# The place of the key norms and the row sums between two pairs of heads, in a decoder layer on one core

## The reference

```
P = layernorm(x) @ W_in + b_in            # 16 heads of Q, K, V, G, 64 wide each
W = (1e-4 + sqrt(max(q2 + k2 - 2 Q K^T, 0))) ** -2    # q2, k2: squared norms
W = W / (1e-4 + sum(W, axis=-1))
H = G * (W @ V)
x = x + H @ W_out + b_out
```

## Time and profile before

| what | value |
|---|---|
| median of 3 runs | 1544.21 us (1541.64 to 1545.7) |
| the profiled execution | 1542.54 us, its span 1540.7 us |
| granted TensorE clock, mean over the span | 0.961 |
| busy: PE, DVE, ACT, POOL | 1389.6, 995.6, 925.9, 600.9 us |
| row sums (L592) | 128 instructions, 32.7 us |
| key norms (L511) into `ps_s` | 240 instructions, 29.6 us |

### The profile page before, as it was taken

One profiled execution on the slowest core, in us unless ns is written; L12 is line 12 of the kernel. 1 busy time (PEld: TensorE's weight loads), 2 busy tenths in 40 slices (PEclk: granted clock), 3 DMA queues, 4 the chain that ended last, 5 costly groups with the idle time before them and its releaser, 6 DMA issues.

```text
span 1540.7 us, 22759 instructions
## 1 busy us (share of the span) xinstructions
PE 1389.6 (90%) x7209; PEld 878.4 (57%) x7210; DVE 995.6 (65%) x1447; ACT 925.9 (60%) x678; POOL 600.9 (39%) x484
## 2 busy tenths in 40 slices
PE   6899999999999999999989558888872999999995
PEld 4555555555555555555546146676661666666664
DVE  7978888888888988898885826666666221212121
ACT  1789999999999999999999412223230122222221
POOL 5344455455545454446441512222221233333331
PEclk9999999999999999999999769999995999999998
DMA  4000000000000000000001323111120143323322
GB/s 145 14 1 15 27 27 14 14 27 27 14 27 14 27 17 24 14 27 14 20 0 27 97 60 111 48 44 51 48 87 18 21 135 95 77 41 89 84 31 72
DMA packets 68828, 67.23 MB, mean 44 GB/s; under 512 B 6752, under 2 KB 61280, under 8 KB 68768
## 3 DMA queue, kind: packets, MB, share of 16 engines
q1 hardware_dynamic: 61504, 56.91, 11.5%
q0 software_dynamic: 7296, 9.97, 3.8%
HBM read 49.03 MB, written 19.92 MB: 45 GB/s over the span
## 4 chain that ended last, share of the span: by engine, by line
PE 67%; issue 14%; DVE 8%; POOL 4%; ACT 4%; DMA 2%; DVEq 0%; POOLq 0%; SPq 0%; ACTq 0%
PE ps_s L564 14%; PE ps_s L823 12%; PE ps_o L579 12%; PE ps_p L467 9%; PE ps_o L848 7%; PE ps_s L467 3%; POOL v_aug L1730 2%; DVE wts L1027 2%; PE ps_s L511 2%; PE ps_p L592 2%; PE ps_p L836 2%; ACT wts L1522 1%; PE ps_s L503 1%; PE ps_o L656 1%; PE ps_o L540 1%
## 5 line engine op out<-in xcount | busy, mean ns | idle before, releaser
L1676 POOL TENSOR_TENSOR v_aug<-v_aug,wts 128x1024 f32<-128x1024 f32 x96 | 232.9, 2426 | 348.0 <-DVE v_aug L1016 347.6
L1027 DVE TENSOR_SCALAR wts<-ps_s,k 128x1024 f32<-128x1024 f32 x240 | 297.0, 1279 | 90.9 <-PE ps_s L564 83.2
L1516 ACT ACTIVATE wts<-wts 128x4096 f32<-128x4096 f32 (+1 forms) x80 | 230.3, 2933 | 53.9 <-DVE wts L1027 32.7
L579 PE MATMUL ps_o<-wts,g_r 128*64 128x512 f32 x1024 | 250.2, 612 | 3.6 <-ACT wts L1524 3.6
L1522 ACT ACTIVATE wts<-wts,eps_d 128x2048 f32<-128x2048 f32 (+1 forms) x96 | 246.2, 2564 | 0.2
L1524 ACT ACTIVATE wts<-wts 128x2048 f32<-128x2048 f32 (+1 forms) x96 | 238.4, 2484 | 3.0
L1436 DVE TENSOR_TENSOR wts<-rinv,ps_s 128x352 f32<-128x352 f32 x76 | 39.6, 521 | 253.5 <-ACT rinv L1593 170.3
L823 PE MATMUL ps_s<-wts,qk 128*128 x608 | 197.6, 468 | 3.1 <-issue 2.3
L823 PEld LDWEIGHTS ps_s<-wts,qk 128*128 128x128 f32 x608 | 110.3, 191 | 64.7 <-issue 16.8
L1593 ACT ACTIVATE rinv<-ps_s 128x352 f32<-128x352 f32 x76 | 35.2, 463 | 176.6 <-PE ps_s L823 176.6
L579 PEld LDWEIGHTS ps_o<-wts,g_r 128*64 128x64 f32 x1024 | 63.3, 137 | 120.8 <-issue 115.0
(11 more groups left out here) (241 smaller groups left out, 2342.3 us busy)
## 6 DMA issues: line engine op xcount, KB each, us to landing
wts<-in_w SPq DMA_DIRECT2D x16, 704.0 KB, 5.4
raw<-in_w_in SPq DMA_DIRECT2D x64, 128.0 KB, 2.3
h_t<-o_raw SPq DMA_DIRECT2D x16, 512.0 KB, 2.7
qk<-h_t SPq DMA_DIRECT2D x16, 512.0 KB, 4.0
wts<-in_w SPq DMA_DIRECT2D x8, 640.0 KB, 7.1
acc<-wts SPq DMA_DIRECT2D x17, 128.0 KB, 1.7
wts<-in_x SPq DMA_DIRECT2D x2, 1024.0 KB, 5.8
wts<-in_x SPq DMA_DIRECT2D x1, 2048.0 KB, 9.1
```

Source lines behind the costliest of these rows:

```text
L579: mm = pe.matmul(ps_o[r, t], v_pair[:, b, r], wts[:, h, b, t], start=b == 0, stop=b == SB - 1)
L1027: dve.tensor_scalar(wts[:, h, b, :], ps_s[:, h, :], k2[:, 2 * b + h:2 * b + h + 1], 0.0, ALU.add, ALU.max).then_inc(S_.max_ok, 1)
L1516: act.activation(chunk(start, end), chunk(start, end), ACT.Sqrt).then_inc(S_.sqrt_ok, 1)
L1676: pool.tensor_tensor(acc_w[:, 0], acc_w[:, 0], wts[:, 0, b], ALU.add).then_inc(S_.add_ok, 1)
```

## The change

TensorE's handoff makes the key norms of pair p + 2 directly behind the transposes of the values, and the row sums of pair p behind them, as the last group ahead of the weighted values of pair p + 1. What each group waits for and signals is unchanged, and so are the programs of the other engines.

```
                     project_g(p + 1, ps_s[:, 1])
                     turn_v(p + 1)
-                row_sums(p, ahead >= 1)
                 if ahead == 2:
                     norm_k(p + 2, ps_s[:, 0])
+                row_sums(p, ahead >= 1)
```

## The result

The changed kernel takes 1576.77 us (median of 4 executions, 1571.07 to 1584.43) against 1543.53 us of the kernel before in the same session: ratio 1.0218, 95% interval 1.0172 to 1.0265. That is 33 us slower; the forecast was 12 us slower, 1556.4 us, with 1567 as the upper end of its range. The profiled execution took 1584.43 us, its span is 1582.6 us.

The account below looks back on a forecast made before the run. TensorE was taken to bound the pair loop. Stalls of 0.55 + 13 x 0.76 less 14 x 0.03 gave +10.0 us, clock falls +2.2; 12.2 in all gave 1556.4 us beside the median, range 1549.5 to 1567.

Parts of the forecast that it names:

- The pause: In front of each handoff's first key norm, TensorE waits for q_n: 0.76 us, in the first handoff 0.55.
- What it costs: Over 14 handoffs, the stalls less 0.03 us each for the distances' shorter wait: +10.0 us.
- Does it pass on, what is queued behind: The stall delays all behind it and recurs each trip; later row sums stay hidden, margins 0.61 and 0.92 us.
- What the earlier key norms give: At VectorE's copy of the key norms, which doesn't wait for them: their earlier end gains 0.
- The clock: Behind the handoff's pause and key norms, the clock falls at one handoff, at most two: estimate +2.2 us.
- the fill's pause: In the fill, 2.73 us idle and then key norms go with a clock fall; over three times the handoff's pause.
- The row at 833.70: Stretch from 833.70 to 847.30, TensorE busy throughout with context matmuls 32 to 77 columns wide, mean clock 0.76.
- rival 1: The clock falls at most handoffs, 34 to 58 us on top of 10.0: 1578 to 1602 us, chance 0.11.
- the forecast's own case: The stall at the handoffs with no clock fall or a few: 1556.4 us, chance 0.80.
- the main line: The stall at the handoffs with no clock fall or a few: 1553.0 to 1567.8 us, chance 0.80.
- Rivals 2 and 3: Stall replaces TensorE's 0.27 us wait: 1550.4 us, chance 0.05; q_n done when TensorE arrives: 1543.8 us, chance 0.04.

Follow-up runs that it names:

- e1_thick: The changed kernel with three 512-column matmuls added between the transposes and the key norms, filling the pause: 1550.33 us, ratio 1.0049.
- e3_pause_first: The kernel before, its order kept, with the wait for q_n put in front of the row sums: 1552.02 us, ratio 1.006.
- e18_elsewhere_thin: e12_thick_elsewhere with six 2-column matmuls added in the pause of the handoff: 1570.1 us.
- e12_thick_elsewhere: The changed kernel with three 512-column matmuls added ahead of the queries' projection, mid-pair, in pairs 1 to 13, the pause left empty: 1570.24 us.
- e6_norms_twice: The kernel before, its order kept, with the key-norm instructions made twice in each of 14 handoffs: 1586.23 us, ratio 1.0292.
- e14_elsewhere_turns: e12_thick_elsewhere with six transposes added in the pause of the handoff: 1558.88 us.
- e5_half_rows: The changed kernel with the row sums cut in two, half ahead of the key norms and half behind them: 1548.6 us, ratio 1.005.
- e4_rows_before_turn: Against the kernel before, row sums moved ahead of the transposes, so key norms follow the transposes without a pause: 1548.83 us, ratio 1.0042.
- e15_elsewhere_rows_first: The order of e4_rows_before_turn with the three mid-pair 512-column matmuls of e12_thick_elsewhere: 1558.79 us.
- e7_split_norms: The changed kernel with the key norms cut in two, four blocks ahead of the row sums and four behind them: 1551.1 us, ratio 1.0074.

## Why the prediction was wrong

- **The pause**: right. 0.76 us in front of the first key norm, released by q_n, in twelve of the 14 handoffs. In the first it was 0.55, as forecast; in the last it was 0.59, which the forecast had taken to be like the others.
- **What it costs**: 0.54 us per trip instead of 0.73 (0.76 less 0.03), and nothing behind the last handoff, where the forecast had counted another 0.73; so 6.8 us instead of 10.0 (6.6 in e1_thick, whose loop has no fall). The row sums take 1.77 us behind the norms instead of 1.87, the weighted values behind the row sums 1.81 up to the distances instead of 1.90. In e3_pause_first, where norms still precede values, the wait costs its full 0.8. The forecast took the groups' times as independent of their neighbours; they are not, by 0.1 us. Why is not shown.
- **Does it pass on, what is queued behind**: right. What is left of the pause lengthens the trips, TensorE's wait for the guards stays at 0.27, and without a fall nobody waits for the row sums. The exception is the stretch behind the last handoff, which is not bound by TensorE.
- **What the earlier key norms give**: nothing, right.
- **The clock**: this is the step that failed, and in it one factor. What a fall costs was right: 1.7 us the short one (52.99 - 51.28), 3.3 the long one (54.60 - 51.28), against 1.7 and 3.4. That there would be falls was right for each of the three profiles of the changed kernel. The count, "one, at most two", was not: 12 in the profiled execution, 32.5 us where the sum had 2.2. The reason given was that the fill's pause was over three times as long. But the length of the pause is the wrong thing to compare: with the pause filled by 2-column matmuls the clock fell as often as with it empty (six of 13 trips in e18_elsewhere_thin and in e12_thick_elsewhere), and with the norms doubled and no pause at all it fell at most handoffs (e6_norms_twice). The norms behind the pause belong to it, and they are nearly as long as in the fill (1.87 us against 2.28). The row at 833.70, where the engine was never idle and the clock still fell, spoke for this; the forecast gave it to rival 1 and left it out of the count.
- **Rival 1**, falls at most handoffs, 1578 to 1602 us, chance 0.11, is what the two profiles of the slower kind and the times show for ten of 14 executions (1571 to 1589). Its ground was partly wrong: what the Trainium skill says of transposes (TensorE: Matmul & The Clock Gate, Part 4) isn't borne out by those here (no fall in e14_elsewhere_turns), while the stretch at 833.70 pointed the right way. Four of the 14 executions, 1553 to 1555 us, are the forecast's own case, and the one of them that was profiled has one fall. So the main line was not wrong about what can happen, but about how often: it had 0.80 and came in four of 14. That the first four executions were all of the slower kind was in part chance: of the next ten, six were.
- **Rivals 2 and 3**: neither occurred.

Left open: what decides, in one execution of the changed kernel, whether falls repeat. In the profile with 12 falls, the trips of 54.60 us follow each other unchanged, and in e12_thick_elsewhere falls come at every other handoff: a fall shifts the next handoff, and the lengths of trips seem to decide whether it meets the same conditions again. That is argued, not shown. Nor is it explained why e5_half_rows has falls, while e4_rows_before_turn and e15_elsewhere_rows_first, with transposes and norms side by side, have none in their profiles and times that leave room for one or two at most. The orders of e3_pause_first and e7_split_norms were not tried with e12's matmuls, so their freedom from falls was seen at one length of trip each.

## What to carry to other kernels

When a wait on the bounding engine is about to lose its cover, look at what stands beside it: here a pause of 0.76 us next to 1.87 us of 2-column matmuls cost up to 3.3 us more through the clock. Read the granted clock of each trip, not only TensorE's busy time, which went up here (50.3 to 53.7 us) while the work stayed the same. And where a kernel can fall into a repeating pattern of clock falls, one execution, or four in one session, doesn't give its time; wide work that fills the pause (0.70 us here) is a cheap test of the cause.

## What was not expected of the hardware

- A TensorE that is busy for 99% of a trip can have its clock lowered: 54.23 of 54.61 us busy at 0.94, with 2-column matmuls in the pause.
- 0.70 us of added work in each of 14 handoffs, with trips of 52 us, made the kernel 13 us faster than it was with the pause left empty: 1557.4 us against 1570.2.
- Transposes of fp32 blocks kept the clock up as 512-column matmuls did (1558.9 against 1557.4 us).
- One program had two outcomes on one chip in one session, 1553.0 and 1577 to 1589 us, with a mean clock over the span of 0.958 and of 0.934 to 0.942.
